# Summing the rows of x on ScalarE instead of VectorE, with the four orders of an iteration laid out again

## The reference, cut to what matters

```python
def L0(x, mask, Wq, Wo):                 # 8 heads of 32, 512 positions, q = k = v
    q = transpose(x) @ Wq.T
    logits = (scale * q @ q.T * cmask + (1 - cmask) * NEG) * rmask
    return transpose(softmax(logits) @ q @ Wo.T)

def L1(x, emb, ...):                     # 16 heads of 32, 256 positions
    xn = rms_norm(x, g_norm) * (1 + scale) + shift
    q, k, v = split(xn @ W_qkv)
    q, k = rms_norm(q, g_q), rms_norm(k, g_k)
    o = softmax(q @ k.T / sqrt(32)) @ v
    return o + o @ W_out

x = x + L0(x, cond, Wq, Wo)
x = x + L1(x, cond, ...)
```

## Time and profile before

| | |
|---|---|
| time of three runs | median 1366.49 us (1365.67 to 1368.57) |
| the profiled execution | 1369.83 us, its span 1367.8 us, mean granted clock of PE 0.961 |
| PE | busy 1265.5 us, 93% of the span |
| DVE | busy 1079.0 us, 79% |
| ACT | busy 770.8 us, 56% |
| POOL | busy 787.5 us, 58% |
| chain that ended last | PE 78%, DVE 11%, ACT 4%, issue 3%, DMA 2%, POOL 1% |
| transfers, from issue to landing (median) | mask CBI 3.4 us, row B0 from NMT 1.8 us, out 3.4 us, residual x 4.8 us |

### The profile page before, as it was taken

The page is one execution under the profiler, slowest core; times in us unless marked ns, Lnnn a source line. Parts: engine busy times, 40 slices in busy tenths (PEclk is TensorE's granted clock), DMA queues, the critical chain, the costliest instruction groups (busy, mean ns, idle before and its releaser), DMA issues.

```text
span 1367.8 us, 20709 instructions
## 1 busy us (share of the span) xinstructions
PE 1265.5 (93%) x6896; PEld 592.0 (43%) x6896; DVE 1079.0 (79%) x932; ACT 770.8 (56%) x1377; POOL 787.5 (58%) x391
## 2 busy tenths in 40 slices
PE   2877899999999999999999999999999999999976
PEld 1523344444444444444444444444444444443432
DVE  5355798888888898888888798888889798888543
ACT  1243657565657666565656656565766656565522
POOL 0232747675674757675674757576574757556622
PEclk8588899999999999999999999999999999999988
DMA  7304251625435261625435261635435172534040
GB/s 247 100 11 126 57 142 38 172 77 130 118 89 145 59 165 40 170 79 128 120 86 146 48 172 47 162 87 122 127 77 147 40 181 52 137 88 109 16 109 15
DMA packets 77702, 142.99 MB, mean 105 GB/s; under 512 B 21280, under 2 KB 22816, under 8 KB 77600
## 3 DMA queue, kind: packets, MB, share of 16 engines
q1 hardware_dynamic: 68880, 126.17, 36.8%
q10 hardware_dynamic: 8720, 15.51, 3.6%
HBM read 32.02 MB, written 8.39 MB: 30 GB/s over the span
## 4 chain that ended last, share of the span: by engine, by line
PE 78%; DVE 11%; ACT 4%; issue 3%; DMA 2%; POOL 1%; ACTq 1%; POOLq 0%; DVEq 0%; SPq 0%
PE PX L440 22%; PE PO L383 9%; PE PS L360 9%; PE PX L467 7%; DVE NM L1043 6%; PE PS L372 5%; PE PO L403 4%; PE PX L307 4%; PE PM L331 4%; DVE NM L1036 3%; PE PM L392 2%; PE PM L458 2%; PE PO L406 2%; PE PX L418 2%; PE PM L340 2%
## 5 line engine op out<-in xcount | busy, mean ns | idle before, releaser
L710 ACT ACTIVATE E<-PS,KBIAS 128x512 f32<-128x512 f32 x512 | 339.1, 687 | 255.1 <-PE PS L360 234.4
L440 PE MATMUL PX<-WQKV,XNT 128*128 128x512 f32 x768 | 399.7, 611 | 15.6 <-ACT XNT L827 12.2
L1036 DVE TENSOR_REDUCE NM<-PM 128x4 f32<-128x2048 f32 x128 | 293.3, 2292 | 100.0 <-PE PM L331 97.0
L1282 POOL TENSOR_TENSOR E<-E 128x1024 f32<-128x1024 f32 x112 | 276.4, 2480 | 162.7 <-PE PO L383 141.0
L1312 POOL TENSOR_TENSOR KQLO<-E 128x1024 f32<-128x1024 f32 x64 | 151.6, 2368 | 253.8 <-ACT E L717 253.8
L360 PE MATMUL PS<-B,A 97*128 97x512 f32 x512 | 282.6, 594 | 9.7 <-ACT E L710 6.3
L1294 POOL TENSOR_TENSOR RQK<-RQK,HALF 128x16 f32<-128x16 f32 x64 | 201.3, 3145 | 38.1 <-DVE RQK L1123 34.8
L717 ACT ACTIVATE E<-PS 128x512 f32<-128x512 f32 x256 | 147.2, 597 | 118.0 <-PE PS L372 108.9
L1043 DVE TENSOR_REDUCE NM<-PM 128x8 f32<-128x2048 f32 x64 | 146.7, 2292 | 40.3 <-PE PM L340 40.0
L440 PEld LDWEIGHTS PX<-WQKV,XNT 128*128 128x128 f32 x768 | 132.8, 192 | 90.9 <-issue 64.3
L360 PEld LDWEIGHTS PS<-B,A 97*128 97x128 f32 x512 | 94.5, 194 | 139.3 <-issue 91.2
(11 more groups left out here) (80 smaller groups left out, 1407.4 us busy)
## 6 DMA issues: line engine op xcount, KB each, us to landing
A<-QHI SPq DMA_DIRECT2D x256, 64.0 KB, 2.0
B<-QHI SPq DMA_DIRECT2D x256, 64.0 KB, 2.0
A<-KQHI SPq DMA_DIRECT2D x128, 128.0 KB, 2.4
B<-KQHI SPq DMA_DIRECT2D x128, 128.0 KB, 2.4
XB<-x SPq DMA_DIRECT2D x16, 512.0 KB, 4.0
A<-QLO SPq DMA_DIRECT2D x128, 64.0 KB, 2.0
B<-QLO SPq DMA_DIRECT2D x128, 64.0 KB, 2.0
X<-x ACTq DMA_DIRECT2D x16, 512.0 KB, 4.8
```

The lines of the kernel that those rows point to most:

```text
L440: last = mm(PX[:, :], XNT[:, c, t * P:(t + 1) * P], WQKV[:, c, part * DM:(part + 1) * DM], start=(c == 0), stop=(c == 3))
L710: fn(E[:, probs(seg, i, g), h, :], PS[n % 2][:, :], ACT.Exp, bias=KBIAS[:, g, b:b + 1], scale=SCALE).then_inc(exp_done, 1)
L1036: v.tensor_reduce(NM0[:, q, :].rearrange("p (h k) -> p h k", k=KB0)[:, :, kb], PM[:, :, :], axis=AX.X, op=ALU.max, negate=True).then_inc(m ...
L1282: g_.tensor_tensor(running(seg, i)[:, heads_, :], running(seg, i)[:, heads_, :], E[:, probs(seg, i, g), heads_, :], ALU.add).then_inc(done, 1)
```

## The change

`sums_x` leaves DVE and goes to ACT. There it is two copies of a half of XB onto itself, each with an accumulated sum; `xs_done` now counts two per image. It stands behind the fourth exp of segment A. The semaphores' other counts and all computations stay as they are.

The four written orders are laid out again:

- PE: the first score stands ahead of `qk(i,0,0)`; `maxima0(i,i,1,...)`, the `qk` products and `heads_rows` are placed anew among the scores of A and B; `weights_summed0("A")` and `values_weighted0("A",3)` stand together; `values_weighted0("B",3)` goes ahead of segment C; `out1` is cut otherwise; `values1` and `maxima0(i+1,0,...)` of segment C come a step later, and `maxima0(i+1,0,3)` comes ahead of `step_c(3,0)`.
- ACT: `round_query(i+1,0)` goes from segment B, step (0,3), to (2,3), so behind `mean0`; `keep_x1` and `load_residual` come some steps earlier, `take_context1(i,..,2)` comes last.
- DVE: `invert1` and `context1` of heads 2 and 3 are spread; `add_eps(1)` comes behind `maxima0(1,3)`; at the turn, `invert1(0)` stands between norm and modulate, `context1(0)` and `split0(i+1,1)` behind modulate.
- POOL: `power_heads(2)` goes ahead of `norm_heads(1)`.

```diff
-        xs_done = ev("xs_done", 1)
+        xs_done = ev("xs_done", 2)
@@ PE
-                if l1:
-                    qk(i, 0, 0)
-
                 step_a(0, 0)
+                if l1:
+                    qk(i, 0, 0)
                 step_a(0, 1)
...
                 step_b(0, 0)
+                if p0:
+                    project0(i, i + 1, 0)
                 step_b(0, 1)
-                if p0:
-                    project0(i, i + 1, 0)
                 step_b(0, 2)
+                if l0:
+                    weights_summed0("A", i, 0)
+                    values_weighted0("A", i, 0, 3)
                 step_b(0, 3)
-                if l0:
-                    weights_summed0("A", i, 0)
+
+                step_b(1, 0)
                 if l1:
                     heads_rows(i, i - 1, 0)
...
+                step_b(3, 3)
                 if l1:
                     maxima1(i, i - 1, 3)
-                step_b(3, 3)
+                if l0:
+                    values_weighted0("B", i, 1, 2)
                 if l1:
                     values1(i, 0, 0, 1)
                     rows1(i, i - 1)
-                if l0:
-                    values_weighted0("B", i, 1, 2)
+                    values1(i, 0, 2)
                 if p0:
                     maxima0(i, i + 1, 0, 0)
-                if l1:
-                    values1(i, 0, 2, 3)
+                if l0:
+                    values_weighted0("B", i, 1, 3)
+                if l1:
+                    values1(i, 0, 3)
...
@@ ACT
+            def sums_x(i, b):
+                act.wait_ge(xin_in.sem, xin_in.at(b))
+                act.wait_ge(p0_full.sem, p0_full.at(b - 1))
+                for c in range(2):
+                    fn(XB[:, c, :], XB[:, c, :], ACT.Copy, accum_out=XS[:, c:c + 1]).then_inc(xs_done.sem, 1)
+
...
                 step_a(0, 2)
                 step_a(0, 3)
+                if p0:
+                    sums_x(i, i + 1)
                 if l1:
                     take_heads(i, i - 1, 0)
...
                 step_b(0, 3)
-                if p0:
-                    round_query(i, i + 1, 0)
                 if l1:
                     round_heads(i, i - 1, 0)
...
                 step_b(2, 3)
+                if p0:
+                    round_query(i, i + 1, 0)
...
@@ DVE
-            def sums_x(i, b):
-                dve.wait_ge(xin_in.sem, xin_in.at(b))
-                dve.wait_ge(p0_full.sem, p0_full.at(b - 1))
-                v.reduce_sum(XS[:, :], XB[:, :, :], AX.X).then_inc(xs_done.sem, 1)
-
...
-                if l1:
-                    invert1(i, i - 1, 0)
                 if l0:
                     residual0(i, i, 0)
                     residual0(i, i, 1)
+                    mean_square(i, i)
+                if p0:
+                    maxima0(i, i + 1, 0, 3)
+                if l0:
+                    norm(i, i)
+                if l1:
+                    invert1(i, i - 1, 0)
+                if l0:
+                    modulate(i, i)
                 if l1:
                     context1(i, i - 1, 0)
-                if l0:
-                    mean_square(i, i)
-                if p0:
-                    maxima0(i, i + 1, 0, 3)
-                if l0:
-                    norm(i, i)
                 if p0:
                     split0(i, i + 1, 1)
-                if l0:
-                    modulate(i, i)
...
@@ POOL
                     power_heads(i, i - 1, 1)
+                    power_heads(i, i - 1, 2)
                     norm_heads(i, i - 1, 1)
-                    power_heads(i, i - 1, 2)
```

More of the change, by code:

```diff
@@ L598, in iteration @@
                     values_weighted0("B", i, 1, 0)
+                step_b(2, 0)
                 if o1:
                     out1(i, i - 2, 0, 3)
+                step_b(2, 1)
                 step_b(2, 2)
+                if l1:
+                    maxima1(i, i - 1, 1)
                 if l0:
                     values_weighted0("B", i, 1, 1)
-                if l1:
-                    maxima1(i, i - 1, 1)
+                if o1:
+                    out1(i, i - 2, 1, 0)
                 step_b(2, 3)
-                step_b(3, 0)
                 if o1:
-                    out1(i, i - 2, 1, 0, 1)
+                    out1(i, i - 2, 1, 1)
                 if l1:
                     maxima1(i, i - 1, 2)
+                step_b(3, 0)
                 step_b(3, 1)
@@ L670, in iteration @@
                     maxima0(i, i + 1, 0, 3)
+                step_c(3, 0)
                 step_c(3, 1)
@@ L951, in iteration @@
                     take_context1(i, i - 1, 0)
-                if p0:
-                    round_query(i, i + 1, 1)
                 step_c(2, 1)
@@ L966, in iteration @@
                     norm(i, i)
-                if l1:
-                    take_context1(i, i - 1, 2)
                 if p0:
@@ L974, in iteration @@
                 step_c(3, 3)
+                if l1:
+                    take_context1(i, i - 1, 2)
             def loads():
@@ L1166, in iteration @@
                     add_eps(i, i - 1, 0)
+                if l0:
+                    maxima0(i, i, 1, 1)
                 if o1:
-                    invert1(i - 1, i - 2, 2)
                     invert1(i - 1, i - 2, 3)
                 if l0:
-                    maxima0(i, i, 1, 1)
                     maxima0(i, i, 1, 2)
@@ L1174, in iteration @@
                     square_sums(i, i - 1, 1)
+                if l0:
+                    maxima0(i, i, 1, 3)
+                if l1:
                     add_eps(i, i - 1, 1)
                 if l0:
-                    maxima0(i, i, 1, 3)
                     add_keys0("A", i, 1, False)
@@ L1183, in iteration @@
                     add_keys0("A", i, 2, False)
+                if o1:
+                    context1(i - 1, i - 2, 2)
+                if l0:
                     add_keys0("A", i, 3, True)
@@ L1188, in iteration @@
                     add_eps(i, i - 1, 3)
-                if o1:
-                    context1(i - 1, i - 2, 2)
                 if l0:
                     take_sums0(i, i, 0)
+                    invert0(i, i, 0, 0)
+                if l1:
+                    split1(i, i - 1, 0)
                 if o1:
@@ L1234, in iteration @@
                     residual0(i, i, 1)
-                if l1:
-                    context1(i, i - 1, 0)
-                if l0:
                     mean_square(i, i)
@@ L1242, in iteration @@
                     norm(i, i)
+                if l1:
+                    invert1(i, i - 1, 0)
+                if l0:
+                    modulate(i, i)
+                if l1:
+                    context1(i, i - 1, 0)
                 if p0:
                     split0(i, i + 1, 1)
-                if l0:
-                    modulate(i, i)
                 if l1:
```

118 lines of the change are left out of this document (48 added, 70 removed).

## The result

The changed kernel took 1394.76 us (median of four runs, 1387.76 to 1410.44) beside 1366.08 us for the kernel before (1364.38 to 1368.57). The ratio is 1.0191, 95% interval 1.0144 to 1.0239: slower, by 1.4 to 2.4%. The highest of the four runs was a disturbed one, and the ratio leaves it out. The forecast of 1367.8 was wrong, and the time lies above its range of 1355 to 1380.

What follows compares the result with a forecast made beforehand. PE (TensorE) bounds the kernel, busy 75.64 of 77.00 us, so only its short waits can be won. Start +4.7, fifteen periods −3.0, end −0.4 make +1.3 on 1366.5: 1367.8 us, range 1355 to 1380.

Steps and rivals of the forecast that it cites:

- the term of the first score ahead of `qk(i,0,0)`: Segment A, PE: 0.23 of a score moves into the wait for XNT, a gain of 0.23 us per period.
- The start: First image: sums on ACT delay the mask 3.7 us, round_query behind mean0 adds 1.0; cost 4.7, bounds 3.4 to 6.
- the estimate by that page: Start, ACT: counting a table-load drain of some 1.38 us, the start would cost 6.1 and the sum stay below 1369.2.
- The sums in the steady part: Moving the sums of x from DVE to ACT is worth nothing in the period, as long as the orders hold.
- Segment B: POOL takes the lock first by 0.4; DVE's add_keys0("B",3) lasts about 3 us, and the segment's gain is given back.
- the half microsecond: Segment B: PE would reach maxima0(i+1,0,0) at place 52.8, half a microsecond sooner, but for DVE's add losing the lock.
- The period: One turn of the loop over segments A to C: 76.85 us, from 77.04; gain 0.2 after POOL's wait of 0.1.
- the 3.0: The fifteen periods together: a gain of 0.2 each, 3.0 us in all.
- GpSimd's chain: POOL's masked_out, pow and norm pieces end later, so PE's head transposes wait 0.1 us a period (0 to 1.0).
- rival C: POOL's chain ends behind PE's arrival at the head transposes: period 77.6, time 1379 at the upper bound; chance 0.19.
- Rival B: Segment B's half microsecond is kept: period falls by 0.7, time 1360.3; chance 0.28.
- The end: Last image: the last exp no longer stands behind take_context1(2), a gain of 0.4 us.

Runs made afterwards that it cites:

- e10: The kernel before with SP's load of x held until the row of maxima has landed, nothing else: 1380.15 us, ratio 1.0104 to before.
- e5: The kernel before with only the sums of x moved to ACT, behind the fourth exp of segment A: 1372.12 us, ratio 1.0019 to before.
- e4: The changed kernel with the sums of x back on DVE, all orders else as changed: 1391.03 us, ratio 1.0182 to before.
- e6: e3 with POOL's last add_keys0 of segment B waiting for DVE's, so DVE gets the lock: 1367.88 us, ratio 1.0008 to before.
- e3: The changed kernel with SP's load of x held until the row of maxima of the image before has landed: 1377.90 us, ratio 1.0071 to before.
- e7: e6 with image 0's sums on DVE and its round_query(0) ahead of mean0, as before the change: 1362.97 us, ratio 0.9953 to before.
- e8: e7 with SP's mask load issued an iteration earlier, ahead of the 24 transfers of stack0(i+1,1): 1357.21 us, ratio 0.9918 to before.

## Why the prediction was wrong, point by point

**The step that failed** is the term of the first score ahead of `qk(i,0,0)`. I had the row of maxima landing 1.8 behind its issue, near 662.5, earlier than XNT, and so 0.23 to win. The 1.8 was the median of a group in the view of DMA, the same before and after:

```profile
B<-NMT ACTq DMA_DIRECT2D x32, 8.0 KB, 1.8
```

That group holds 32 transfers, the sixteen of the turn and sixteen from the middle of a segment, where no load of x is under way. The median is right for one half and silent on the other. The trace of the kernel before would have told, had I asked it for the spread of this line:

```profile
L754 ACTq DMA_DIRECT2D B<-NMT x32: 509/526/597, 35.1 to 1230.8; - x32
...
DMA to landing us min/median/max: 1.8/1.8/4.8
```

The same view, asked for one transfer at a time, gives 1.8 to 4.8 over turns 2 to 14, 2.8 in the mean. The very row, issued at 660.66, landed 2.9 later, near 663.6 and not 662.5: behind XNT, which was whole at 662.74. In ten of these thirteen turns the row landed later than XNT, and only the product that stood ahead of the score hid it. In the kernel after it is 2.6 to 4.3, 3.2 in the mean: there x is issued 1.4 to 2.3 ahead of the row, before 1.6 to 3.2.

In two turns of the kernel before the product did not hide it all. One of them, timeline of the kernel before:

```profile
737.84 0.53 ACTq L754 DMA_DIRECT2D B<-NMT  x1
...
742.72 0.71 PE L360 MATMUL PS<-B,A 97*128 97x512 f32 x2 [1.60 <-issue]
```

This landing took 4.8. The view gives the 1.60 no releaser, and so the list of waits for the row has only one of 0.6, at 72.33 in image 0. The other such turn has 0.85 at 1129.82, 4.1 behind its row. The periods behind the two are 78.90 and 79.73, where the prediction counted on 77.04 in all. With the load of x held (e10) the score starts 2.7 behind the row's issue in the same two turns, and both gaps are gone.

What the step cost: the waits for the row and for XNT together are 16.7 more than before (29.5 − 0.6 − 12.2), 1.1 a turn lost where 0.23 was to be won. 16.7 + 4.7 on the median of before gives 1387.9, at the lower end of what was measured. The periods cost 11.8 in the profiled runs, so the other orders gave some 5 back in spite of the lock.

**The start** was right. The forecast put the end of both sums at 14.55 and the first product 3.7 later, at 17.4. The timeline of the kernel after:

```profile
12.09 1.28 ACT L712 ACT_TABLE_LOAD   x1 [12.09 <-issue]
13.38 0.63 ACT L712 ACTIVATE XB<-XB 128x512 f32<-128x512 f32 x1
14.87 2.48 POOL L1262 TENSOR_TENSOR XB<-XB,CBM 128x512 f32<-128x512 f32 x2 [13.36 <-ACT XB L712]
17.60 3.72 PE L307 MATMUL PX<-XB,WQ 128*128 128x512 f32 x4 [17.60 <-POOL XB L1262]
26.83 0.51 PE L331 MATMUL PM<-QHI 32*128 32x512 f32 x4 [1.03 <-ACT QHI L679]
...
55.36 1.20 PE L360 MATMUL PS<-B,A 97*128 97x512 f32 x2
```

It is 3.9 at the first product, 5.1 at the first maxima and at the first real score (50.28 before), and 4.7 at the first `qk`, against the forecast's 3.7 and 4.7. The first activation starts 0.01 behind the table load. The drain that the Trainium skill counts with a table load (ScalarE: Activation LUTs, What ACT_TABLE_LOAD costs) does not show here, so the estimate by that page, 1.4 more, did not come true.

**The sums in the steady part** are worth nothing, as said: e5 shows unchanged periods (77.19 in the mean, before 77.33), and e4's time is that of the kernel after within the intervals.

**Segment B** was right in mechanism and direction. The lead that decides was forecast as 0.4 and is 0.43 in most images (0.16 in the turn shown above), VectorE's add was forecast as about 3 and takes 2.98 to 3.29 from image 2 on, GpSimd's as 2.35 and takes 2.35. The earlier trace rows show an unusual image: VectorE is ahead by 0.37 there, in most images of the kernel before by 0.1, and GpSimd's add takes 3.3. The prediction took GpSimd's place from the sum of its five pieces, 10.95, and not from that row, whose 714.41 is 11.2 behind the visit and would have left a lead of 0.1; the sum was the better guide. The Trainium skill's rule on the shared port (SBUF — State Buffer, SBUF: two separate sides), which it gives for GpSimd instructions that read SBUF, as this one does, fits the trace: VectorE's add ends 1.08 behind the end of GpSimd's. The loss was a little larger than the half microsecond that it was to eat: the waits are 0.65 to 0.68 in twelve of 14 places, and e6 against e3 puts it at 0.62 a period in undisturbed turns (76.25 and 76.87) and at 0.67 in the mean of fifteen (76.75 and 77.42).

**The period** of 76.85, which rests on segments A to C together, is what e3 shows in undisturbed turns, 76.87, beside 77.04 in those of before: the 0.2 that was forecast. But only about half of e3's periods are so; in the mean of fifteen it has 77.42, no less than before's 77.33, so holding the load of x alone doesn't bring the 3.0.

**GpSimd's chain** (rival C) was priced at 0.1 a period, 0 to 1.0. In the kernel after it hardly shows (7.0 in four places). In e7 it is 8.5 in nine places; there SP is held for the row, and PE is no longer 2 us late at the turn, and which of the two brings it out was not told apart. The early mask load took 5.8 us off the median (e7 to e8). That is 0.4 a period, inside its bounds and above my choice, though only 2.4 of the 5.8 can be read from undisturbed periods. **Rival B**'s price of 0.7 a period compares with the 0.62 to 0.67 of the lock; its outcome of 1360.3 was passed only with the row, the lock, the start and the mask mended together (1357.21).

**The end** was to bring 0.4 and cost 1.7 in the profiled run, in which the granted clock was 0.74 between 1318 and 1338, where the answering stretch before (1301.5 to 1321.5) had 0.83. What part of the 1.7 is order and what is clock was not told apart; in e3, with the same order at 0.83, the end took 86.1 against 86.3 before. The difference between the medians (28.7) is larger than that of the profiled runs (18.2), and the rest of it stays open: the profiled run is the lowest of the four, and the next two lie 4.5 and 9.5 us above it.

## What to carry to other kernels

A median landing time over a group of transfers says nothing about the one that is issued behind a large load: before putting work in front of a wait, ask the trace for the landings of that very transfer, turn by turn, look at what else is issued in the 3 us ahead of it, and use the worst landing seen there. A gap without a named releaser behind a transfer that is usually hidden can be that transfer. When a queue is given a new wait, follow everything behind it in its order; here a hold that mended one place cost 1% through a mask load that stood behind it. An order that loses can hold a gain: this one was 1.9% slower as it stood, and 0.8% faster than before with the load of x, one lock, the start and one mask load mended.

## What the hardware showed unexpectedly

- A transfer of 8 KB lets its reader start 1.87 behind the issue when no load of x is under way (e8, turn 15 of the kernel after, and 12 of 14 turns of e3; in the other two it was 3.05, for a reason that stays open), and 2.7 to 4.4 behind it when a load of 512 KB from another queue was issued 1.4 to 2.3 before.
- After a stall of PE the granted clock can fall for several matmuls. In the turn at 751.86 of the kernel after, behind 2.27 without work, the busy view of the next stretch shows it at 0.50, the lower of the two levels (1.2 GHz); two products took 1.91 instead of 1.02. In turns 2 to 15 without this one the same products took 1.02 to 1.09, even behind the longest stall (3.29, at 439.15), so the length of the stall alone does not decide. Columns of the row: stretch, length, busy us of PE, PEld, DVE, ACT and POOL, clock, DMA share, GB/s.

```profile
751.80:755.00 3.20, 3.14 (x5) 1.83 (x6) 2.06 (x2) 0.89 (x2) 1.81 (x1) 0.50 0.33 82
```

- Two elementwise adds that meet cost the later one the whole rest of the earlier one, down to a lead of 0.16 us: which of two engines pays can hang on a difference that no sum of prices resolves.
